# Moving one of two output combinations from step 4 to step 7 of a body, and its transposes from step 6 to step 10

## What is computed

```python
x = x + conv3x3(group_norm(x), W)              # 64 -> 64 channels
t = tokens(x)                                  # 3136 tokens of 64 numbers per image
t = t + attention(layer_norm(t), Wq, Wk, Wv)   # one head, softmax over 3136 keys
t = t + experts(layer_norm(t))                 # 16 experts, the best 2 of each token, weighted by its gates
```

## Time and profile before

| | |
|---|---|
| Median of 3 runs | 2684.65 us (2683.14 to 2685.62) |
| Profiled execution, its time | 2681.76 us |
| Profiled execution, span from first to last instruction | 2680.0 us |
| Mean granted TensorE clock, share of full speed | 0.963 |
| TensorE busy | 2432.0 us, 91% of the span |
| VectorE busy | 1807.4 us, 67% |
| ScalarE busy | 1300.9 us, 49% |
| GpSimd busy | 1012.5 us, 38% |

### The profile page before, as it was taken

One profiled execution on the slowest core, in us unless ns is written; L12 is line 12 of the kernel. 1 busy time (PEld: TensorE's weight loads), 2 busy tenths in 40 slices (PEclk: granted clock), 3 DMA queues, 4 the chain that ended last, 5 costly groups with the idle time before them and its releaser, 6 DMA issues.

```text
span 2680.0 us, 46785 instructions
## 1 busy us (share of the span) xinstructions
PE 2432.0 (91%) x13821; PEld 1636.8 (61%) x13821; DVE 1807.4 (67%) x5891; ACT 1300.9 (49%) x2986; POOL 1012.5 (38%) x1097
## 2 busy tenths in 40 slices
PE   5899999999999999999999999999999999996763
PEld 3566556666666666666666666666666666564662
DVE  5577777766677676676776777676766776774432
ACT  2344444454545555454545555455555555453542
POOL 2022015200444325342444324442444324365665
PEclk8899999999999999999999999999999999997875
DMA  3043001111212212121212222222222111222442
GB/s 80 23 105 89 22 25 51 47 38 36 65 55 55 56 45 67 53 61 47 63 51 62 49 56 62 59 55 51 56 55 59 36 49 53 54 59 62 122 98 49
DMA packets 226561, 152.98 MB, mean 57 GB/s; under 512 B 100241, under 2 KB 216721, under 8 KB 226321
## 3 DMA queue, kind: packets, MB, share of 16 engines
q1 hardware_dynamic: 190880, 98.26, 14.0%
q0 software_dynamic: 31456, 48.03, 7.5%
q10 hardware_dynamic: 3984, 3.70, 0.6%
HBM read 83.92 MB, written 65.27 MB: 56 GB/s over the span
## 4 chain that ended last, share of the span: by engine, by line
PE 66%; DVE 13%; issue 5%; POOL 1%; ACT 1%; DMA 0%; POOLq 0%; SPq 0%; DVEq 0%; ACTq 0%
PE ps_o L1493 17%; PE ps_s L1481 9%; PE ps_m L1453 8%; PE ps_s L1482 7%; PE ps_x L1652 4%; PE ps_z L1519 4%; PE ps_z L1666 3%; DVE max_part L1132 3%; PE ps_z L1641 2%; DVE ln_c L1045 2%; PE ps_x L1659 1%; PE ps_y L1572 1%; PE ps_s L1652 1%; PE ps_y L1556 1%; DVE up L1303 1%
## 5 line engine op out<-in xcount | busy, mean ns | idle before, releaser
L1132 DVE TENSOR_REDUCE max_part<-ps_m 128x1 f32<-128x448 f32 x1400 | 851.9, 620 | 600.9 <-PE ps_m L1453 591.4
L964 ACT ACTIVATE prob<-ps_s 128x448 f32<-128x448 f32 x1400 | 758.3, 544 | 599.0 <-PE ps_s L1482 568.0
L1493 PE MATMUL ps_o<-prob,v_s 128*64 128x448 f32 x2800 | 625.7, 555 | 0.0
L794 POOL DMA_INDIRECT got<-sorted_y,slot x448 | 425.6, 950 | 465.0 <-PE ps_s L1482 264.3
L1481 PE MATMUL ps_s<-q_a,k_a 128*128 128x448 f32 x1400 | 586.7, 419 | 2.4 <-ACT prob L964 0.8
L773 POOL DMA_INDIRECT sorted_x<-xn,slot x448 | 425.9, 951 | 430.1 <-PE ps_s L1482 228.9
L1453 PE MATMUL ps_m<-k_a,q_a 128*128 128x448 f32 (+3 forms) x1600 | 536.9, 362 | 45.3 <-DVE max_part L1132 38.9
L1482 PE MATMUL ps_s<-q_b,k_a 128*128 128x448 f32 x1400 | 512.3, 366 | 0.0
L1453 PEld LDWEIGHTS ps_m<-k_a,q_a 128*128 128x128 f32 (+1 forms) x1600 | 296.8, 188 | 128.8 <-DVE max_part L1132 97.1
L1493 PEld LDWEIGHTS ps_o<-prob,v_s 128*64 128x64 f32 x2800 | 179.1, 136 | 277.8 <-issue 245.1
L1481 PEld LDWEIGHTS ps_s<-q_a,k_a 128*128 128x128 f32 x1400 | 265.3, 189 | 116.8 <-issue 94.0
(11 more groups left out here) (186 smaller groups left out, 2972.9 us busy)
## 6 DMA issues: line engine op xcount, KB each, us to landing
fx<-sorted_x SPq DMA_DIRECT2D x43, 384.0 KB
sorted_y<-fy SPq DMA_DIRECT2D x42, 320.0 KB
xh<-in_x SPq DMA_DIRECT2D x96, 126.0 KB
fx<-sorted_x SPq DMA_DIRECT2D x47, 256.0 KB
sorted_x<-fy POOLq DMA_DIRECT2D x28, 320.0 KB, 6.0
sorted_x<-xn,slot POOLq DMA_INDIRECT x448
got<-sorted_y,slot POOLq DMA_INDIRECT x448
x_now<-in_x SPq DMA_DIRECT2D x112, 56.0 KB
```

Source lines behind the costliest of these rows:

```text
L794: g.indirect_dma_start(out=got[k % 2][m][:, j, :], out_offset=None, in_=sorted_y[b % 2][0:GROUPS[group_of(k)].room * SLOTS], in_offset=bas ...
L964: a.activation(prob[(at.n * KEY_TILES + i) % PROBS][:], ps_s[(at.n * KEY_TILES + i) % 2][:, 0:CHUNK], ACT.Exp).then_inc(s["p_ready"], 1)
L1132: v.tensor_reduce(max_part[n % 2][0:here.stop - here.start, j, kb:kb + 1], ps_m[(passes_before(n) + m) % 2][0:here.stop - here.start, 0:CH ...
L1493: t.matmul(ps_o[side:side + CHANNELS, 0:CHUNK], v_s[u % 2][:, i, :], prob[(n * KEY_TILES + i) % PROBS][:], start=(i < 2), stop=(i >= KEY_T ...
```

## The change

Place 0 is moved in both tables: VectorE's combination from step 4 to step 7, TensorE's transposes and ScalarE's copy from step 6 to step 10. Places 1 and 2 stay.

```diff
-COMBINE_AT, COMBINED_AT = (4, 18, 21), (6, 21, 23)
+COMBINE_AT, COMBINED_AT = (7, 18, 21), (10, 21, 23)
```

## The result

| | before | after |
|---|---|---|
| Median, ten runs each (us) | 2684.28 (2680.78 to 2688.11) | 2695.04 (2688.88 to 2707.95) |
| Ratio, 95% interval | | 1.0047 [1.0032, 1.0062] |
| Profiled execution, time and span (us) | 2681.76 and 2680.0 | 2693.94 and 2692.2 |
| Mean granted TensorE clock in it | 0.963 | 0.966 |

The kernel is slower, by 0.47%: 0.0047 x 2684.28 = 12.6 us, with 8.6 to 16.6 by the interval. The median, 2695.04 us, lies in the wider range forecast, 2690 to 2719 us, but 2 us under the forecast's own range of 2697 to 2711 us; the middle of 18.4 us was too high. The profiled executions differ by 12.2 us.

A forecast was written before the change was run, and what follows sets the result against it. TensorE's queue was taken to bound the kernel. Fourteen bodies 17.1, chunk 1 of the last image 0.3, the end -2 and the clock 3 gave 18.4 us: 2703 us, own range 2697 to 2711, wider 2690 to 2719.

The forecast's parts named there:

- The bank's order: At step 10 the transposes into ps_y wait for q_b, then L1565 waits for their copy: 1.37 us.
- four signs: L1580 waits about 1.1 us, L1565 0.2 to 0.4; step 5 to L1565 14.8; step 8's reduction straight behind combination.
- The body: One chunk of one image: 1.37 - 0.15 = 1.22 us longer, bounds -0.15 and 2.75 us.
- fourteen bodies: Bodies in images 2 to 6 having first-place combinations with convolution and queries beside them; 17.1 us longer in total.
- VectorE at no cost: VectorE's combination, 1.66 us, fits into 1.90 us of idle time around steps 8 and 9; cost nothing.
- The clock: TensorE falling to 1.2 GHz behind the new waits: two falls in fourteen, 3 us; bounds 0 and 21 us.
- The end: Behind the last image, where TensorE waited 2.08 us for the combination: -2 us, bounds 0 and -4 us.
- The sum: 17.1 + 0.3 - 2 + 3 = 18.4 us over the kernel before; 2703 us on the median.
- the clock falls often: Rival: seven to fourteen falls of TensorE's clock instead of two add 8 to 18 us, 2711 to 2725 us; chance 0.16.
- part is given back: Rival: ScalarE's copy is hidden or chunk 6 bodies absorb their cost, 2690 to 2697 us; chance 0.12.

The follow-up runs named there:

- the last image alone: Steps 7 and 10 only in image 7 and behind it, the old 4 and 6 elsewhere, against the kernel before: 2680.71 us, ratio 0.9991.
- the kernel with the double copy: The changed kernel with ScalarE copying place 0's transposes twice, first to a tile nobody reads: 2721.79 us, ratio 1.0144 to the kernel before.

## Why the prediction was right, and where its sum was off

**The bank's order: right.** Its four signs came as written: L1580 waits for q_b (1.01 us; about 1.1 forecast), L1565 waits for out_s (0.20; 0.2 to 0.4), step 5 to L1565 takes 1489.18 - 1474.33 = 14.85 us (14.8), and the reduction of step 8 follows the combination. Only the transposes cost it, and a change of bank alone takes the cost away with every step left where the change put it; this is shown by experiment, not argued.

**The body: 1.29 us measured, 1.22 forecast.** Its two terms were the removal at step 6 (0.15 forecast; 0.32 - 0.21 = 0.11 measured, since L1529 now waits 0.50 us for x_conv) and the stretch from L1580 to the next taker (1.37 forecast from another place of the body, 1.39 measured). Over fourteen bodies 18.1 against 17.1 us. That bodies of chunk 6 would not get any of it back at their wait of step 17 was right too: the four with that wait are 1.30 to 1.36 us longer once the clock is taken out.

**VectorE at no cost: right.** The 1.90 us of idle time took the 1.66 us. The kernel with only the transposes moved shows the rest: VectorE's move costs nothing in the fourteen, and earns its part in the last image.

**The clock: mis-sized.** I took two falls in fourteen, +3 us. Behind the new waits there is none in the fourteen bodies after, and none in the two other kernels with the same waits that were traced: 0 of 42. At old waits fewer bodies fell than in the profile of before, -4.1 us. That part moves from run to run: the ten runs after lie 19 us apart (2688.88 us at a mean clock of 0.971, 2707.95 at 0.959), those of before 7. So the term is about nothing at the new wait in the three executions that were traced; what the slowest runs did there is not known, and the profile's own difference at the old waits is no property of the change that I could show. By the Trainium skill's rule ("TensorE: Matmul & The Clock Gate", "Part 4: PE-mode transpose": transposes don't count as busy for the clock as matmuls do) most of the fourteen would have fallen, as the prediction reckons. That did not come: four transposes follow a wait of 1.01 us, four more one of 0.20 us, and the clock stays full. Whether they count less than matmuls no run here tests.

**The end: mis-sized.** -2 us forecast with bounds 0 and -4; the profile has -0.4 - 0.4 - 4.5 = -5.3. I had counted GpSimd's wait of 1.89 us, which did go, down to the 0.30 us that every issue has. I had not counted that the 2.08 us wait of the earlier trace rows is followed by the lower clock, which goes with it. Not all 4.5 us need be the change's: the four traces with the fall take 236.4 us behind the attention in the mean, the six without it 232.9, so 3.6 us is my estimate for the move. The runs of the last image alone, -2.4 us with -5.6 to +0.5 by the interval, don't decide between these sizes.

**The sum.** 18.1 + 0.2 - 5.3 = 13.0 us without the clock and the stretch ahead of body 0, against the 12.6 [8.6, 16.6] of the runs. That these agree to 0.4 us is closer than the interval can tell. The forecast's 18.4 is 3 too high by the clock, 3 by the end, and 1 too low by the bodies. Two of the rivals' ranges don't follow from their own terms: "the clock falls often" ends at 2703 + 18 = 2721 us and not 2725, and "part is given back" at 2695 and not 2697. Of the rivals, "part is given back" named the time that came (2690 to 2697 us), by a mechanism that did not: the copy isn't hidden, and the chunk 6 bodies pay like the others.

## What to carry to other kernels

When a step moves, write down, for every buffer it takes, who had it last and who takes it next at the new place, and read from the trace when the one's reader ends and how long the other's start lies behind; here that gave 1.22 of 1.29 us per body, while the work moved (0.3 us of transposes, 1.7 us on VectorE) cost nothing. A step that must be late is better given a buffer without such neighbours, or put where the engine waits anyway, than put at the first free step. And look for long waits near the clock's falls: a fall cost 1.2 to 3.2 us, but it follows a wait only in some executions, so one trace with it and one without don't show that a change removed it.

## What the runs showed of the hardware that I had not expected

The clock term is a matter of degrees, and steep. With idle times of 1.01 and 0.20 us close behind each other no body of 42 fell (three traces); with 1.01 and 0.63 us five of 14 fell, for up to 3.2 us each (one trace); with one of 2.26 us (2.43 in n = 40) eight of 14, for 1.6 us each (one trace). So 0.43 us more of waiting cost 0.43 us in most bodies and 2.1 to 3.6 us in some, and a wait could not be priced by its own length. The old waits lie between: the one of 1.25 us in chunk 3 was followed by a fall in 7 of 60 bodies of all ten traces, the one of 1.7 us in chunk 6 in 9 of 32. Why bodies with the same waits differ stays open: n = 19 and n = 33 of the kernel with the double copy have the same 1.01 and 0.63 us, and only the second fell.
